# Gated delta stage of a hybrid block: where the outputs' mean square is summed

## The reference, cut to what matters

```python
h = _rmsnorm(x, norm1_w)
q = _short_conv_silu(h @ Wq, conv_q_w).reshape(B, T, H, dk)     # 4-tap causal convolution, then SiLU
k = _short_conv_silu(h @ Wk, conv_k_w).reshape(B, T, H, dk)
v = _short_conv_silu(h @ Wv, conv_v_w).reshape(B, T, H, dv)
q, k = _l2norm(q) * dk ** -0.5, _l2norm(k)
def step(S, inp):                                               # scanned over the tokens
    q_t, k_t, v_t, g_t, b_t = inp
    S = S * jnp.exp(g_t)[..., None, None]
    delta = (v_t - jnp.einsum('bhk,bhkv->bhv', k_t, S)) * b_t[..., None]
    S = S + jnp.einsum('bhk,bhv->bhkv', k_t, delta)
    return (S, jnp.einsum('bhk,bhkv->bhv', q_t, S))
o = _rmsnorm(o, onorm_w) * jax.nn.silu((h @ Wg).reshape(B, T, H, dv))
x = x + o.reshape(B, T, H * dv) @ Wo
```

## Time and profile before

| | |
|---|---|
| median of 3 runs | 3792.14 us |
| lowest and highest | 3787.14 and 3795.1 us |
| time of the profiled execution | 3798.17 us |
| its span, first to last instruction | 3795.2 us |
| mean granted TensorE clock | 0.951 |
| busy over the whole span | PE 3294.0 us (87%), DVE 2723.1 (72%), ACT 2038.1 (54%), POOL 1804.8 (48%) |

### The profile page before, as it was taken

The page is one execution under the profiler, slowest core; times in us unless marked ns, Lnnn a source line. Parts: engine busy times, 40 slices in busy tenths (PEclk is TensorE's granted clock), DMA queues, the critical chain, the costliest instruction groups (busy, mean ns, idle before and its releaser), DMA issues. The chain is left out here.

```text
span 3795.2 us, 87218 instructions
## 1 busy us (share of the span) xinstructions
PE 3294.0 (87%) x32714; PEld 2466.9 (65%) x32714; DVE 2723.1 (72%) x5753; ACT 2038.1 (54%) x4599; POOL 1804.8 (48%) x1647
## 2 busy tenths in 40 slices
PE   4789999999999999968999999986898599899998
PEld 3577777777777777745666566654666366656665
DVE  5577777777777777647777677775999477767775
ACT  3456565656565656513666366632444366636662
POOL 3355555555555555434666166632122466526662
PEclk8689999999999999989999999997999799999999
DMA  4111111111111111033122321222112222131122
GB/s 123 23 24 25 25 25 25 26 25 26 24 27 24 27 25 24 11 95 81 43 53 56 93 50 44 71 79 55 47 50 55 63 49 64 45 95 44 46 71 70
DMA packets 409630, 182.71 MB, mean 48 GB/s; under 512 B 235808, under 2 KB 384384, under 8 KB 406656
## 3 DMA queue, kind: packets, MB, share of 16 engines
q1 hardware_dynamic: 409216, 177.15, 19.0%
HBM read 94.47 MB, written 40.12 MB: 35 GB/s over the span
## 5 line engine op out<-in xcount | busy, mean ns | idle before, releaser
L1197 POOL TENSOR_TENSOR delta_cv<-delta_cv,delta_last_tap 96x256 f32<-96x256 f32 (+1 forms) x384 | 332.7, 867 | 623.4 <-DVE delta_cv L1631 623.4
L1938 POOL TENSOR_TENSOR g_a_rn<-g_a_clip,g_minus_half 128x16 f32<-128x16 f32 x64 | 186.4, 2912 | 271.2 <-DVE g_a_clip L2202 243.0
L1938 POOL TENSOR_TENSOR f_a_rn<-f_a_clip,f_minus_half 128x16 f32<-128x16 f32 x64 | 186.3, 2911 | 260.7 <-DVE f_a_clip L2202 232.5
L2155 ACT ACTIVATE g_a_pr<-g_ps,g_a_nb,g_a_rn 128x128 f32<-128x128 f32 x512 | 185.5, 468 | 146.4 <-DVE g_a_nb L2236 146.4
L2155 ACT ACTIVATE f_a_pr<-f_ps,f_a_nb,f_a_rn 128x128 f32<-128x128 f32 x512 | 185.5, 468 | 146.4 <-DVE f_a_nb L2236 146.4
L1466 ACT ACTIVATE delta_cv<-delta_ps,delta_conv_qk 96x256 f32<-96x256 f32 x256 | 120.9, 472 | 253.5 <-PE delta_ps L1299 252.7
L1623 DVE SCALAR_TENSOR_TENSOR delta_cv<-delta_ps,delta_conv_qk,delta_cv 96x256 f32<-96x256 f32 x256 | 122.1, 477 | 169.5 <-ACT delta_last_tap L1468 169.2
L1243 PE MATMUL delta_ps<-delta_state,delta_qk 96*128 96x192 f32 x1024 | 199.4, 339 | 27.3 <-issue 22.8
L1623 DVE SCALAR_TENSOR_TENSOR delta_cv<-delta_ps,delta_conv_v,delta_cv 128x256 f32<-128x256 f32 x192 | 92.1, 480 | 155.5 <-ACT delta_last_tap L1468 154.1
L1243 PEld LDWEIGHTS delta_ps<-delta_state,delta_qk 96*128 96x128 f32 x1024 | 168.3, 193 | 41.7 <-issue 38.1
L1466 ACT ACTIVATE delta_cv<-delta_ps,delta_conv_v 128x256 f32<-128x256 f32 x192 | 90.5, 471 | 127.5 <-PE delta_ps L1299 127.5
(11 more groups left out here) (350 smaller groups left out, 10477.3 us busy)
## 6 DMA issues: line engine op xcount, KB each, us to landing
f_a_vm<-f_a_v SPq DMA_DIRECT2D x128, 130.0 KB, 2.3
g_a_vm<-g_a_v SPq DMA_DIRECT2D x128, 130.0 KB, 2.3
delta_gd<-delta_dram_row SPq DMA_DIRECT2D x16, 1024.0 KB, 4.6
window_vm<-window_v SPq DMA_DIRECT2D x64, 128.0 KB, 2.3
f_m_x<-y SPq DMA_DIRECT2D x24, 256.0 KB, 3.5
delta_dram_inv<-delta_sub SPq DMA_DIRECT2D x16, 256.0 KB, 2.1
f_m_more<-x SPq DMA_DIRECT2D x16, 256.0 KB, 3.9
x<-f_m_x SPq DMA_DIRECT2D x16, 256.0 KB, 2.3
```

The lines of the kernel that those rows point to most:

```text
L1197: pool.tensor_tensor(cv[0:M, t % 3], cv[0:M, t % 3], last_tap[0:M, t % 3], ALU.add).then_inc(summed.sem, 1)
L1938: pool.tensor_tensor(rn[:, u % 2], clip[:, u % 2], minus_half[:], ALU.pow).then_inc(rn_sb.sem, 1)
L2155: e = act.activation(pr[:, u % 2, half, i, :], ps[:, score_bank(u, half), i * P:(i + 1) * P], ACT.Exp, bias=nb[:, u % 2, half, i:i + 1], s ...
```

## The change

The squares of four heads, one instruction before, become four instructions of one head each, which also leave the sum of their row in `ostat[:, 0, h]` (`accum_out`). DVE's two sums per chunk go. The counter of the statistics has one step per chunk in place of three. The waits follow: ACT's squares now wait for POOL's `of` of the chunk before (which comes after DVE's L1613, the reader of the sums that they overwrite), and DVE's L1613 waits for ACT's squares in place of DVE's own sums.

```diff
-    ostat_step = mark("ostat_step", 3)
+    ostat_sb = mark("ostat_sb")
...
-                    ostat_step.need(pool, C)
+                    ostat_sb.need(pool, C)
                     o_normed.need(pool, C - 1)
                     pool.tensor_tensor(of[:], ostat[:, 1, :], minus_half[:, 0:H], ALU.pow).then_inc(of_sb.sem, 1)
...
                     o_sb.need(act, C, i + 1)
                     up_ps.need(act, C, i + 1)
-                    mine = slice(HB * i, HB * i + HB)
-                    act.activation(vr[:, C % 3, mine], o[:, C % 2, mine], ACT.Square).then_inc(osq_sb.sem, 1)
+                    of_sb.need(act, C - 1)
+                    for h in heads(i):
+                        e = act.activation(vr[:, C % 3, h, :], o[:, C % 2, h, :], ACT.Square, accum_out=ostat[:, 0, h:h + 1])
+                    e.then_inc(osq_sb.sem, 1)
...
                             bvr_sb.need(act, n)
-                            ostat_step.need(act, C - 3, 2)
+                            osq_sb.need(act, C - 3)
...
-                    ostat_step.need(dve, C - 2)
+                    ostat_sb.need(dve, C - 2)
...
-                for i in range(2):
-                    C = chunk(t, 11 + i)
-                    if C is not None:
-                        osq_sb.need(dve, C, i + 1)
-                        mine = slice(HB * i, HB * i + HB)
-                        dve.tensor_reduce(ostat[:, 0, mine], vr[:, C % 3, mine], AX.X, ALU.add).then_inc(ostat_step.sem, 1)
                 C = chunk(t, 12)
                 if C is not None:
                     of_sb.need(dve, C - 1)
-                    ostat_step.need(dve, C, 2)
+                    osq_sb.need(dve, C)
                     q_eps_sb.need(dve, C)
                     dve.scalar_tensor_tensor(out=ostat[:, 1, :], in0=ostat[:, 0, :], scalar=1.0 / DV, in1=q_eps[:, C % 2],
-                                             op0=ALU.mult, op1=ALU.add).then_inc(ostat_step.sem, 1)
+                                             op0=ALU.mult, op1=ALU.add).then_inc(ostat_sb.sem, 1)
```

## The result

| | before | after |
|---|---|---|
| median, 20 runs each | 3790.58 us | 3801.53 us |
| lowest and highest | 3786.47 and 3796.08 | 3785.26 and 3814.32 |
| ratio, 95% interval | | 1.0027 [1.0016, 1.0038] |
| time of the profiled execution, its span | 3798.17, 3795.2 | 3801.52, 3798.6 |
| mean granted TensorE clock | 0.951 | 0.947 |

The account below looks back on a forecast made before the run. PE, 90% busy, was taken to set the pace, with DVE's relief hidden by POOL. Seven units losing 1.0 us each (+7.0) and one clock fall (+3.45) gave +10.5 on 3792.1: 3802.6 us, range 3776 to 3828.

Parts of the forecast that it names:

- DVE's sums: Late half: PE's 1.63 us wait for kd goes but returns before L1308, hidden by POOL's solve chain; gain nothing.
- Squares of the late half: Ahead of the step-16 work that starts POOL's chain: up to 1.85 us of growth hidden, cost nothing.
- the first group of the early half: Step 2, full-clock units: ACT then waits 1.49 us for PE, so growth up to 1.49 us is hidden.
- Squares of step 3: Early half, full clock: uncovered; growth, taken as 1.0 us, delays the `ot` copy and PE's L1408 by as much.
- Who pays: Seven full-clock units lose 1.0 us each, +7.0; in low-clock units slow PE hides growth up to 1.48 us.
- The clock: Idle time at L1408 among small products drops one of the seven units to the lower clock: +3.45 us.
- rival 2: Fewer low stretches because units lie otherwise in time: 3782 us if five of seven go, 3775 if all; chance 0.13.
- Rival 1: Added idle time makes PE's clock fall in every unit: +31 us, growth then hidden, 3823 us; chance 0.22.
- main case: Relief hidden by POOL, step-3 growth paid in seven units, one clock fall: 3802.6 us, 3794 to 3812; chance 0.38.
- The total: Whole kernel: +7.0 and +3.45 give +10.5 us, 3802.6 us against the median of 3792.1.
- Rival 3: DVE's relief counts: PE's 1.63 us wait goes in fifteen units, not handed on; -17 us, 3775; chance 0.10.
- Rival 4: Nothing on the path: read-out nearly free, PE's 0.17 us is all there is; 3792 to 3795 us; chance 0.17.

Follow-up runs that it names:

- relief_alone: Kernel before with DVE's sums left out and the wide square kept, mean square not computed: 3789.28 us, 0.9978 of before.
- late_half_only: Kernel before with the change made for even chunks alone (squares in steps 16 and 17): 3790.47 us, 0.9984 of before.
- growth_alone: Kernel before with the narrow squares, their sums read out into a spare tile, DVE's sums kept: 3804.25 us, 1.0022 of before.
- late_second: Changed kernel with only the second group's squares put last in their step, behind the `ot` copy: 3789.47 us, 0.9986 of before.
- narrow_only: Kernel before with four Squares of 192 per group, no accumulator, DVE's sums kept: 3785.83 us, 0.9985 of before.
- pool_relief_alone: Kernel before without DVE's sums, squares wide, mean square not computed, two POOL powers moved out of its solve chain: 3732.22 us, 0.9844 of before.
- early_half_only: Kernel before with the change made for odd chunks alone (squares in steps 2 and 3): 3797.67 us, 1.0014 of before.

## Why the prediction was right, point by point

- **DVE's sums.** Their removal was priced at nothing, "hidden by POOL". Right: relief_alone has the projection 16.29 us after L1182 (16.34 before) and PE's wait there grown from 2.70 to 4.4 us (66.5 / 15). The forecast had 4.3. Of the 1.63 us per unit that it gave the relief without that cover, 1.04 came with POOL's chain shortened and a part of the cover left.
- **Squares of the late half, and the first group of the early half.** Priced at nothing, with 1.85 and 1.49 us of cover. Right: late_half_only shows no loss in the late half, and ACT's wait at 910.14 took up 0.65 us.
- **Squares of step 3.** The place and the chain were right: square, product, `ot` copy, L1408. growth_alone carries the whole loss, late_second removes it by moving the second group alone. The **size was off**: 1.0 us taken, 0.65 measured, 0.28 for the split and 0.37 for four read-outs. The step that failed is that "a read-out has to follow its own square and can't overlap it". In the rows it does follow its square's start (by 0.27 us), but it overlaps the end of its own square (913.82), and the next square starts 0.09 us after it, while it still runs; a head takes 0.35 us all told (913.46 to 914.51, three heads in 1.05). From the figures of the Trainium skill, ScalarE: Activation LUTs, section What ACT_TABLE_LOAD costs, the estimate for the split was 0.28 us. narrow_only agrees with it, with 0.28 measured; the read-out was what lay outside it.
- **Who pays.** The forecast let only the seven full-clock units pay. L1408 waits 0.81 us in all fifteen units after, because the clock now falls at L1408 itself and no longer some microseconds ahead of it. Long units became shorter all the same (95.5 against 96.1), since their low stretch shrank from 10.3 to 6.8 us.
- **The clock.** One more long unit was assumed, at 3.45 us. The profiled execution has two more, at 3.85. That the added wait would bring more low stretches in the early half was right in direction for this change (two more), but growth_alone, with the same wait, has only one more there. The premise, that idle time among the small products makes the clock fall, holds at most in part: narrow_only has 0.27 us more idle time there and fewer low stretches. The runs fit rival 2's mechanism better, the position of one unit against the one before, but none tested it alone. By its own sign (units in another order point to rivals 1 and 2) this part of the main case failed: the strict turn-taking is gone.
- **The total.** 7 x 1.0 + 3.45 = 10.5 forecast; 3.3 - 3.6 + 7.7 = 7.4 found in the trace, 10.9 in the medians. The total is nearer than its terms, which were too large in growth and too small in clock. The closeness is luck, then: had the units kept their old turn-taking, 0.65 us in seven of them would have cost 4.6 us, under the 0.2% that can be told from nothing.
- **The rivals.** Rival 1 (all units fall): no, five of thirteen keep the clock; but the runs reach up to 3814 us, and growth_alone has eleven long ones, four of them through the late half. Rival 2 (faster through fewer low stretches): not for this change, but it is what happens in narrow_only. It counted seven low stretches, where seven short units of fifteen leave eight. Rival 3 (relief counts): refuted for this kernel by relief_alone; with POOL's chain shorter the relief does count, at 1.04 us per unit. The Trainium skill, Perfetto Trace Analysis, section Optimizing Scalar/DVE Operations, says that such a move may make sense when DVE is saturated. The trace of relief_alone disagrees (DVE was busy 11.58 of 12.00 us from 866 to 878 us in before, and a short unit gained 0.08 us), and that of pool_relief_alone agrees (1.04 us). Rival 4 (nothing): excluded by the interval, whose lower end, 1.0016, is above the 3795 us of that rival.
- **Waits and counters.** The new wait for `of` never shows in the waits of ACT; priced at nothing, and that holds.

## What to carry to other kernels

A saving on a full engine is worth what the next-latest input leaves of it. Look for that input before pricing the saving: here a POOL chain could give two instructions up, and the change that cost 11 us became part of one that gains 51. Where work grows on an in-order engine, the place in that engine's order decides what the growth costs: look for the copy that another engine waits for, and put the growth behind it, and then check that nothing of it has come to stand ahead of the next such copy. And where a small edit shifts a kernel whose TensorE clock changes in a pattern, count the units at each level before you credit or blame the edit itself.

## What the runs showed of the hardware

- ScalarE's accumulator is read out by a separate instruction, 192 ns long on average, that starts about 0.27 us after its square did and overlaps the next square. At 192 elements it adds 0.09 us per instruction to the queue (1.52 against 1.15 us for four).
- The granted clock fell at 916.9 us after PE had waited 0.81 us at L1408 among 32- and 64-wide products, and stayed full one unit later after the same wait of 0.82 us. Nothing in the single wait tells the two apart. Whether the units before do, no run tested.
- The share of long units isn't steady in the unit's length: 6 of 13 at a short unit of 91.65 us, 4 of 13 at 91.91, 9 at 92.23 (early_half_only), 11 at 92.24 (growth_alone, four of them through the late half), 8 at 92.30, 10 at 92.45. A unit 0.26 us longer gave a faster kernel. A long unit costs 3.2 (95.49 - 92.31) to 4.5 us (96.08 - 91.63) more than a short one, so this pattern moves the time as much as the edit. Why the pattern settles as it does stays open; no experiment set the unit's length by itself, without moving a wait.
- With POOL's chain as it was, the first two units of the delta stage took from 183 us (late_half_only) to 194 us (before) in the profiled executions. What sets them was not tried.
